# A fused S6 + mixture-of-experts layer: the orders of all engines laid out anew, and the norms' shift moved from GpSimd and ScalarE to VectorE

## The reference

```python
x = x + s6(layernorm(x))        # W_in 512x128, conv of 4 taps, 256 hidden, 16 states, rank 64
x = x + moe(layernorm(x))       # 8 experts of width 176, top 2, and a shared part of width 352
# s6:  u, o = x @ W_in.T ; u = silu(conv(u) + b) ; g = u @ W_gate.T -> delta_lo, b, c
#      delta = softplus(delta_lo @ W_delta.T + bias)
#      h_t = exp(A * delta_t) * h_(t-1) + (delta_t * u_t) b_t ;  y_t = h_t . c_t
#      y = (ys + D * u) * sigmoid(o) * o ;  out = y @ W_out.T
# moe: softmax over 8 logits, top 2 renormalised times 2.5;
#      silu(x @ wg) * (x @ wu) @ wd for all experts, weighed, plus the shared part
# layernorm: (x - mean) / sqrt(var + 1e-5)
```

## Time and profile before

| | us | share |
|---|---|---|
| profiled execution | 1347.99 | |
| its span | 1346.3 | |
| TensorE busy (matmul) | 1160.7 | 86% |
| GpSimd busy | 1142.5 | 85% |
| VectorE busy | 1126.5 | 84% |
| ScalarE busy | 1044.9 | 78% |

### The profile page before, as it was taken

One profiled execution on the slowest core, in us unless ns is written; L12 is line 12 of the kernel. 1 busy time (PEld: TensorE's weight loads), 2 busy tenths in 40 slices (PEclk: granted clock), 3 DMA queues, 4 the chain that ended last, 5 costly groups with the idle time before them and its releaser, 6 DMA issues. The chain is left out here.

```text
span 1346.3 us, 26240 instructions
## 1 busy us (share of the span) xinstructions
PE 1160.7 (86%) x9075; PEld 930.5 (69%) x9075; DVE 1126.5 (84%) x1762; ACT 1044.9 (78%) x2155; POOL 1142.5 (85%) x536
## 2 busy tenths in 40 slices
PE   3455999999999989999999999999999999998787
PEld 2323777777777777777777777777777777776677
DVE  3466799999998999899988989989889998898853
ACT  3877788888888788888887888888888888887742
POOL 3299799999999999999999999999999999999820
PEclk8767899999999999999999999999999999998899
DMA  4343323434343224443332333333432334333000
GB/s 109 108 101 88 85 72 86 100 100 104 73 103 97 74 77 100 103 100 81 95 103 70 79 99 100 100 87 90 103 81 74 93 100 100 91 78 98 5 5 9
DMA packets 71486, 115.09 MB, mean 85 GB/s; under 512 B 8173, under 2 KB 30394, under 8 KB 71354
## 3 DMA queue, kind: packets, MB, share of 16 engines
q1 hardware_dynamic: 67178, 110.71, 32.4%
q10 hardware_dynamic: 4176, 2.70, 0.7%
HBM read 41.04 MB, written 5.24 MB: 34 GB/s over the span
## 5 line engine op out<-in xcount | busy, mean ns | idle before, releaser
L405 POOL TENSOR_TENSOR inject<-rep,bc 128x1024 f32<-128x1024 f32 x256 | 604.1, 2384 | 10.7 <-DMA rep<-dd 9.9
L414 POOL TENSOR_TENSOR read<-state,bc 128x1024 f32<-128x1024 f32 x224 | 529.1, 2377 | 35.7 <-DVE state L689 28.1
L689 DVE TENSOR_TENSOR_SCAN state<-decay_ps,inject 128x1024 f32<-128x1024 f32 x224 | 508.3, 2281 | 27.7 <-ACT decay_ps L483 25.3
L483 ACT ACTIVATE decay_ps<-rep,neg_a 128x255 f32<-128x255 f32 x1024 | 423.1, 460 | 27.1 <-DVE state L689 24.8
L923 PE MATMUL work_ps<-xn2T_part,ffn_gate 128*128 128x256 f32 x1344 | 218.7, 300 | 46.2 <-ACT g_silu L471 39.4
L471 ACT ACTIVATE g_silu<-work_ps 128x512 f32<-128x512 f32 x224 | 134.5, 601 | 133.1 <-PE work_ps L923 111.6
L923 PEld LDWEIGHTS work_ps<-xn2T_part,ffn_gate 128*128 128x128 f32 x1344 | 182.0, 195 | 77.8 <-ACT g_silu L471 55.0
L957 PE MATMUL acc_ps<-ffn_down,features 128*128 128x128 f32 (+1 forms) x1792 | 229.0, 277 | 0.0
L957 PEld LDWEIGHTS acc_ps<-ffn_down,features 128*128 128x128 f32 (+1 forms) x1792 | 213.0, 191 | 4.5
L707 DVE TENSOR_TENSOR features<-g_silu,work_ps 128x512 f32<-128x512 f32 x224 | 152.2, 680 | 75.2 <-ACT g_silu L471 40.1
L932 PE MATMUL work_ps<-xn2T_part,ffn_up 128*128 128x256 f32 x1344 | 197.6, 287 | 0.0
(11 more groups left out here) (138 smaller groups left out, 1394.4 us busy)
## 6 DMA issues: line engine op xcount, KB each, us to landing
rep<-dd SPq DMA_DIRECT2D x256, 256.0 KB, 4.7
bc<-bc_rows SPq DMA_DIRECT2D x64, 512.0 KB, 4.8
x_in<-in_L_attn_x_dram SPq DMA_DIRECT2D x32, 128.0 KB, 2.1
out_dram<-result SPq DMA_DIRECT2D x32, 128.0 KB, 1.8
bc_rows<-g_sb SPq DMA_DIRECT2D x32, 32.0 KB
state<-in_L_ffn_w_gate_dram ACTq DMA_DIRECT2D x1, 704.0 KB, 4.4
read<-in_L_ffn_w_up_dram ACTq DMA_DIRECT2D x1, 704.0 KB, 5.9
ffn_down<-in_L_ffn_w_down_dram ACTq DMA_DIRECT2D x1, 704.0 KB, 6.9
```

Source lines behind the costliest of these rows:

```text
L405: pool.tensor_tensor(inject[:, at % RI], du_all, b_all, ALU.mult).then_inc(inject_done, 1)
L414: pool.tensor_tensor(read[:, at % RR], state[:, at % RS], c_all, ALU.mult).then_inc(read_done, 1)
L483: last = act.activation(decay_ps[:, at % 2, j, 1:T], rep[(HALVES * n + half) % RP][:, j, 0, 1:T], ACT.Exp, scale=neg_a[:, col:col + 1])
L689: dve.tensor_tensor_scan(to, decays, inject[:, at % RI].rearrange("p j t -> p (j t)"), 0.0, ALU.mult, ALU.add).then_inc(state_done, 1)
```

## The change

Orders and waits alone, but for one operation: `neg_mean` on ScalarE and the product on GpSimd go, and VectorE does both in one `scalar_tensor_tensor` (mean * -1 * rstd) once a step, between the gating of y and the second weighing. `ln_small` counts one per step now rather than two. Some waits that repeat one already waited for are issued once. The moves, shortened:

- GpSimd: read 2 goes ahead of inject 4, inject 5 ahead of read 3.
- ScalarE: the first cast of xnT stands between decays 2 and 3, the second between 3 and 4; the logarithm of the variance stands ahead of delta's; rstd ahead of decays 5; xn2, z's exponential and z + 1 ahead of decays 6; the transposed xn2's casts ahead of decays 0 of the next sequence. The casts of the FFN weights (once) go from behind silu 2 to behind z's Abs.
- VectorE: see below.
- TensorE: the transposes of xn ahead of the projection and of sum 0; gates 4 ahead of the transposed weights; conv behind sum 2; spread 2 ahead of z; spread 4 ahead of down 0; down 10 and the logits ahead of spread 5; then sums 5 and 6, ups 0, gates 0.

```diff
 # GpSimd, body
+                    if g == 0:
+                        pool.wait_ge(rep_in[half], 16 * JB * (n + 1))
...
                 reads(1)
+                reads(2)
                 injects(4)
-                reads(2)
+                injects(5)
                 reads(3)
-                injects(5)
                 injects(6)
                 injects(7)
-                if on(3) or on(-1):
-                    pool.wait_ge(ln_rstd, k + 4)
-                    pool.tensor_tensor(shift[:], neg_mean[:], rstd[:], ALU.mult).then_inc(ln_shift, 1)
...
 # ScalarE
-                if on(3) or on(-1):
-                    act.activation(neg_mean[:], mean_var[:, :, 0], ACT.Copy, scale=-1.0).then_inc(ln_small, 1)
...
+                if on(3) or on(-1):
+                    act.wait_ge(ln_small, k + 4)
+                    act.activation(rstd[:], log_var[:], ACT.Exp, scale=-0.5).then_inc(ln_rstd, 1)
                 if on(0):
                     decays(k, 5)
...
 # VectorE (moves, with the shift)
+                if on(0):
+                    scan(0)
                 pairs(0)
-                if on(0):
-                    scan(0)
-                pairs(1)
                 if on(-1):
                     take_y(k - 1, 1)
+                pairs(1)
                 pairs(2)
                 if on(0):
                     scan(1)
...
+                if on(0):
+                    scan(2)
+                if on(-2):
+                    dve.wait_ge(comb_steps, 6 * f + 2)
+                    dve.tensor_reduce(picked_sum_ps, picked[:], AX.X, ALU.add).then_inc(comb_steps, 1)
...
+                if on(0):
+                    scan(4)
                 pairs(4)
+                if on(0):
+                    read_own_group()
                 pairs(5)
                 pairs(6)
+                if on(-2):
+                    weigh(0)
                 if on(0):
                     take_y(k, 0)
-                if on(-2):
-                    weigh(0)
+                if on(3) or on(-1):
+                    dve.wait_ge(ln_rstd, k + 4)
+                    dve.scalar_tensor_tensor(out=shift[:], in0=mean_var[:, :, 0], scalar=-1.0, in1=rstd[:], op0=ALU.mult,
+                                             op1=ALU.mult).then_inc(ln_shift, 1)
+                if on(-2):
                     weigh(1)
+                    weigh(2)
                 if on(0):
                     scan(5)
-                if on(-2):
-                    weigh(2)
...
                 if on(-2):
                     weigh(3)
-                if on(0):
-                    scan(6)
+                    weigh(4)
...
                 if on(0):
+                    scan(6)
                     scan(7)
                 if on(-2):
-                    weigh(4)
                     weigh(5)
```

More of the change, by code:

```diff
@@ L591, in body @@
                     act.activation(z_e[:], z_ps, ACT.Abs).then_inc(z_abs_done, 1)
[L592 to L598, removed]
-                if on(0):
-                    decays(k, 6)
+                if on(1) and not on(0):
+                    act.wait_ge(ffn_loaded, 16 * len(ffn_loads))
+                    act.wait_ge(padded, 2)
+                    act.copy(ffn_gate[0][:], gate_staged).then_inc(ffn_high, 1)
+                    act.copy(ffn_up[0][:], up_staged).then_inc(ffn_high, 1)
                 if on(-1):
@@ L627, in body @@
                 if on(1):
+                    decays(k + 1, 0)
                     decays(k + 1, 1)
@@ L726, in pairs @@
                             gated_up(p)
[L728 to L735, removed]
                 if on(0):
                     scan(0)
-                pairs(1)
+                pairs(0)
                 if on(-1):
                     take_y(k - 1, 1)
+                pairs(1)
                 pairs(2)
@@ L786, in body @@
                                       ALU.subtract).then_inc(comb_split, 1)
-                if on(0):
-                    scan(2)
-                    scan(3)
+                if on(3):
+                    n = k + 3
+                    dve.wait_ge(stats_done, n + 1 + count(k - 1))
+                    dve.wait_ge(ln_small, k + 3)
+                    for j in range(TILES):
+                        dve.bn_aggr(mean_var[:, j, :], stats1[:, j, :]).then_inc(ln1_var, 1)
                 if on(-1):
                     n = k - 1
[L792 to L795, removed]
                     dve.wait_ge(x1_done, n + 1)
@@ L964, in body @@
                     gates(1, f)
-                    pe.wait_ge(silu_done, pair(0))
-                    ups(1, f)
                 if on(-1):
@@ L969, in body @@
                 if on(-2):
+                    pe.wait_ge(silu_done, pair(0))
+                    ups(1, f)
                     pe.wait_ge(h_done, pair(0))
@@ L993, in body @@
                         down(chunk, f - 1)
+                if on(2):
+                    n = k + 2
+                    if on(1):
+                        pe.wait_ge(gate_done, k + 2)
+                    pe.wait_ge(ln1_done, n + 1)
+                    for j in range(TILES):
+                        last = pe.matmul(xnT_ps[:, j * P:(j + 1) * P], xn[:, j, :], ident[:], start=(j == 0), stop=False,
+                                         skip_group_check=True)
+                    last.then_inc(xnT_mm, 1)
+                    pe.wait_ge(xnT_high, n + 1)
+                    pe.matmul(xnT_ps, neg_identr[:], xnT_parts[0][:, TAPS - 1:], start=False, stop=True,
+                              skip_group_check=True).then_inc(xnT_rest, 1)
                 if on(-1):
@@ L1006, in body @@
                 if on(0):
+                    pe.wait_ge(result_done, count(k - 2))
                     pe.wait_ge(y_taken, HALVES * k)
-                    pe.wait_ge(result_done, count(k - 2))
                     sum_states(k, 0)
-                if on(2):
-                    n = k + 2
-                    if on(1):
-                        pe.wait_ge(gate_done, k + 2)
-                    pe.wait_ge(ln1_done, n + 1)
-                    for j in range(TILES):
-                        last = pe.matmul(xnT_ps[:, j * P:(j + 1) * P], xn[:, j, :], ident[:], start=(j == 0), stop=False,
-                                         skip_group_check=True)
-                    last.then_inc(xnT_mm, 1)
-                    pe.wait_ge(xnT_high, n + 1)
-                    pe.matmul(xnT_ps, neg_identr[:], xnT_parts[0][:, TAPS - 1:], start=False, stop=True,
-                              skip_group_check=True).then_inc(xnT_rest, 1)
-                if on(-2):
+                if on(-2):
+                    if on(-1):
+                        pe.wait_ge(x1_done, k)
+                    else:
+                        pe.wait_ge(silu_done, pair(3))
+                    gates(4, f)
                     pe.wait_ge(comb_split, 2 * f + 2)
@@ L1075, in body @@
                     ups(6, f)
+                    pe.wait_ge(silu_done, pair(6))
+                    spread_comb(0)
                 if on(0):
@@ L1125, in body @@
                 if on(-2):
+                    down(7, f)
                     down(8, f)
@@ L1133, in body @@
                     down(9, f)
[L1134 to L1135 removed]
+                    down(10, f)
                 if on(-1):
@@ L1166, in body @@
                     ups(0, n)
-                if on(-2):
-                    down(10, f)
+                    pe.wait_ge(xn2T_low, n + 1)
+                    if k == 1:
+                        pe.wait_ge(ffn_ready, PARTS)
+                        pe.wait_ge(ffn_loaded, 16 * len(ffn_loads))
+                    if on(-2):
+                        pe.wait_ge(hc_done, COMBS * f + 5)
+                    else:
+                        pe.wait_ge(x1_done, k)
+                    gates(0, n)
             steps(body)
```

118 lines of the change are left out of this document (50 added, 68 removed).

## The result

The changed kernel takes 1370.12 us, the median of four runs from 1364.28 to 1374.22. The kernel before took 1346.99 beside it (1346.78 to 1347.88). The ratio is 1.0167 with a 95% interval of 1.013 to 1.0205: slower by 23 us. The profiled execution took 1370.09 us with a span of 1368.4, 22.1 over the span before.

The account below looks back on a forecast made before the run. No engine alone was taken as the bound (each 82 to 92% busy), but the order of their waits. Span 1346.3 + 15 (28 passes) - 1 (start) + 0.5 (end) = 1361, stated as 1360; range 1296 to 1370.

Parts of the forecast that it names:

- the mechanism named as likeliest: VectorE's shift, both inputs in SBUF, held for most of a GpSimd product each pass: 1350 to 1369 us, chance 0.50.
- The order alone: Loop pass with the new orders and a shift costing 0.1 us: 37.0 us, 1.3 under before.
- scan 0 to scan 2: First stretch of a pass on VectorE, with pair 0 now behind scan 0: scan 2 starts at 10.3 us.
- scan 2 to the shift: Second stretch of a pass, through GpSimd's read 2 and TensorE to pair 6: 14.5 us, VectorE nearly full.
- the end of the shift to the next scan 0: Third stretch of a pass on VectorE, with scans 5 to 7, weighings and ranking: 12.1 us.
- The wait ahead of pair 2: New VectorE wait in the first stretch, for gate chunk pair 2 from TensorE: 1 us a pass.
- One sign: In the new profile, GpSimd would have no wait over 0.5 us except ahead of reads 2 and 6, for scans.
- The shift: VectorE's shift comes 0.4 us after inject 7 starts on GpSimd and is held 2.0 us; pass 38.8 us.
- GpSimd keeps the port over consecutive operations: Rival: the shift gets in only where GpSimd stops, at read 5; pass 41.1 us, about 1425 in all; chance 0.05.
- The start: Before the steady passes: earlier first inject -2.5, transposes of xn -2, held subtractions +3.5; together -1 us, within 4.
- The end: The two steps after the last scan: +0.5 us, within 3 either way.
- first at the port: Rival: VectorE arrives before inject 7 starts, or the shift isn't held; pass 37.0, 1305 us; chance 0.35 for both.

Follow-up runs that it names:

- a2: The changed kernel with the shift as four one-element tensor_scalar on VectorE, rstd read as a per-partition scalar: 1301.28 us, ratio 0.966.
- a6: a1 plus one unread four-element scalar_tensor_tensor on VectorE in the shift's place, second input in PSUM: 1305.67 us, ratio 0.968.
- a5: a1 plus one unread four-element scalar_tensor_tensor on VectorE in the shift's place, both inputs in SBUF: 1358.14 us, ratio 1.0071.
- a3: The changed kernel with the shift one operation earlier, ahead of y's gating: 1351.76 us, ratio 1.0024.
- a7: a2 with ScalarE's casts of the FFN weights back where they were before the change: 1301.21 us, ratio 0.9659.
- a1: The changed kernel's new orders, with the negated mean back on ScalarE and the shift's product back on GpSimd: 1305.48 us, ratio 0.968.
- b2: The kernel before with its old orders, only the shift moved to VectorE, as four one-element tensor_scalar behind scan 5: 1364.25 us, ratio 1.0115.
- a4: The changed kernel with its one-operation shift 1.2 us later, behind the next weighing: 1329.23 us, ratio 0.984.
- b1: The kernel before with its old orders, only the shift moved to VectorE, as one operation behind scan 5: 1443.14 us, ratio 1.070.

## Why the prediction was right, step by step

1360 was forecast and 1370.12 came, by the mechanism named as likeliest: the shift is held for most of a product in every pass. The size is less good than the mechanism. The time lies at the upper edge of the range (1370), the loss is 23 us where 13 was forecast, and two of the three terms came out right by errors that cancel.

- *The order alone: 37.0 a pass forecast, 36.8 measured* (a2: 26 passes in 955.9 us, 36.76 each; a6: 36.82). The stretches of the changed kernel hold too: scan 0 to scan 2 takes 10.08 us (615.82 - 605.74; 10.3 forecast), scan 2 to the shift 14.37 (14.5), the end of the shift to the next scan 0 11.74 (644.22 - 632.48; 12.1). The wait ahead of pair 2 is 0.60 rather than 1 us, that ahead of scan 2 0.55 (0.5). One sign failed: GpSimd was to have no wait over 0.5 us but ahead of reads 2 and 6, and it stands 1.07 ahead of read 5 and not at all ahead of read 2.
- *The shift: 0.4 us too late forecast and held 2.0; in the trace under 0.1 too late and held 2.3.* a5 and a6 show that two inputs in SBUF are the cause. The pass was to be 38.8 and is 38.50; of the hold 0.4 us is made up (a5 against a6), where 0.2 was forecast. The place was nearer to the boundary than forecast: with a margin of under 0.1 us it could as well have come out as a3 did.
- *GpSimd keeps the port over consecutive operations* had 5 of 100 as a rival for every pass. It is neither the rule nor absent: it happened in 4 of 26 passes at 2.3 to 2.4 us each, 9.4 us together, and brought the mean to 38.87 (1010.6 us / 26). The passes thus added 15.6 us against 15 forecast: the usual pass is 0.3 us shorter than forecast, and the four long ones, which were in no term, make up for it. That is luck. These passes likely make the runs spread too (10 us, 1 us before), since their number can differ; that was not counted over runs.
- *The start*: -0.6, -1 forecast, and again not by its parts. Two of them hold. The first inject came at 57.30, as forecast, and the subtractions took over 2.5 us:

```profile
58.45 3.08 DVE L815 TENSOR_TENSOR ffn_gate<-state,ffn_gate 128x1792 fp32r<-128x1792 f32 x1 [9.57 <-ACT ffn_up L594]
61.46 4.16 DVE L817 TENSOR_TENSOR ffn_up<-read,ffn_up 128x1792 fp32r<-128x1792 f32 x1
```

  Together they are worth +0.9 at sequence 3 (a2 reaches it at 164.05, a7, without both, at 163.19; +1 forecast). But the orders alone bring 3.9 us up to there (a7 against 167.05) where 2 were forecast, and the shift is held in these first passes too, which the sum didn't have: +2.4 (166.41 against a2's 164.05).
- *The end: +0.5 forecast, within 3; measured +7.1.* This term was mis-sized and is most of the ten us missing. I had not gone through the last passes with the hold in them, which meets the shift there too (1.62 us at 1251.61, 2.13 at 1288.30). But the hold can't be all: a5, held 1.58 and 3.27 us in its last passes, has an end of 109.2 us at a granted clock of 0.92, only 2.4 over a1's 106.8. In the changed kernel the clock over the end is 0.84 (0.94 before), and TensorE's busy time, 8.1 us more, is the one that grew. So this looks like TensorE at the lower clock; why the clock fell was not tested.
- *The rival "first at the port" was priced rightly and conditioned wrongly.* 1305 is what the orders give without a hold (1301 to 1306 in a1, a2, a6). But "it has only to be 0.4 us earlier" is false: 0.3 us ahead of the end of inject 6 a3 lost the boundary often enough to come out 50 us over a2.

The profile's verdict against the change fell on one operation. The orders are worth -43 to -47 us (a1, a2), and the shift as one instruction with two SBUF inputs adds 65 to 69 to them.

## What to carry to other kernels

Before an operation moves to VectorE beside a busy GpSimd, look where its inputs lie: with both in SBUF it costs what is left of GpSimd's running instruction, at times a whole one more, however small it is itself, and every operation behind it pays. Give it an input in PSUM, or, for one element at a time as here, make the second one a per-partition scalar, before you shift it about in the order: its place only changes how much is left. And where an engine stands for long, ask what it would do next: with the 43 us that GpSimd stood for rstd gone, b2 had it stand longer for the scans and for rep.

## What the runs showed of the hardware that was not expected

- A held VectorE instruction isn't sure of its turn when GpSimd's product ends: rows of 4.62 to 4.64 us over two products in the changed kernel (4 of 27 in the steady part), of 3.4 us in a4 (3 of 27), and 0.33 or 2.64 us from the same position in a3. In b1 it always had its turn: all 28 held rows from 167.61 to 1279.23 ended with the first product, though the next one followed without a gap each time. What makes the difference is open.
- A per-partition scalar in SBUF beside a one-element input is not held (144 of 198 to 214 ns), while in the preamble a 128x128 operation with such a scalar was the earlier trace rows. Whether that is the input's size or the preamble's work on GpSimd, no run here tells.
- The hold goes both ways: four products of GpSimd took 12.8 us beside VectorE's two subtractions, and 9.3 without.
- With short holds in it, b1 had a granted clock of 0.91 over 200 us in which b2 had 1.00, and in the changed kernel each of the four passes with a doubled hold has 0.96 where the other passes between 204 and 1214 us have 1.00; whether the holds' waits led to it was not tested.
